# The opening of an attention and feed-forward kernel: x loaded tile by tile, normalised rows made ahead, clears and table loads moved

## The chip, the cores and the metric

The kernel runs on one core of a Trainium2 chip. The time is that of one execution on the device, in microseconds. Five engines work side by side, each with its own queue of instructions in fixed order: TensorE (PE, matmuls), VectorE (DVE), ScalarE (ACT), GpSimd (POOL) and SyncE (SP, which here issues all transfers). They wait for one another through counting semaphores.

## The reference, cut to what matters

Input x has 1024 rows of 512 floats. All arithmetic is in float32. The layer is

```
x = x + attention(layernorm(x))      # 32 heads of 128, 8 key/value heads, rotary positions, causal
x = x + ffn(layernorm(x))            # x W^T + b, and a low-rank part weighted by a router
layernorm(x) = (x - mean(x)) / sqrt(var(x) + 1e-5)
q = x w_q, k = x w_k, v = x w_v, lq = x w_lq, lk = lq w_lk, lv = x w_lv    # x here is normalised
out = softmax(mask(q k^T)) v  w_o  +  softmax(mask(q lk^T)) lv  w_lo
```

Only the first layernorm and the projections for the first head belong to the part of the program that the change touches.

## The kernel before

Every float32 operand of a matmul is split in two: a high half (a copy, made by ScalarE, written as fp32r) and a low half (the difference, made by VectorE or GpSimd). A product is three matmuls: high by low, low by high, high by high (lines 414 to 416, `mm3`). So each operand that TensorE reads has to pass ScalarE, and then VectorE or GpSimd.

The program has an opening, eight groups of four heads written out one after another, and a closing part. The order on each engine is that of the source; nothing is scheduled by a program. x lives in `acc`, 8 tiles of 128 rows (`NT` = 8, half of them is `TPC` = 4). The opening does this:

- SP issues the first half of x (`load_x(0)`, L310, 1 MB, one transfer), the identity matrix `ident`, the first weights w_q and w_k, the second half of x, then the constants cos, sin and mask (512 KB each), then w_lq, w_v, w_lk and w_lv. `load` (L321) puts weights into two slots of `stage`; from the third load on it waits until the low half made from the slot is done.
- VectorE: `statistics` (L909 to L917) of four tiles, then ScalarE's square root (`root`, L706), then `inverse_std` (L923 to L927), five tiny operations in a chain. `normalise` (L944) writes a normalised tile into `o_raw`, which has two places, and waits for the transpose that last read its place. `normalised_lo` (L950) makes the low half of the transposed tile.
- TensorE: `normalised_transpose` (L429) turns one tile into `bankT`, which has two banks, by four 128x128 transposes; from the third tile on it waits for the low half of the tile two before. ScalarE's `normalised_hi` (a copy, L701) makes the high half in `xnT`.
- Then TensorE makes eight projections of twelve matmuls each: Q, K, latent Q and V for columns 0 to 511 (n = 0), then the same for columns 512 to 1023 (n = 1). Tiles 4 and 5 are transposed after the first projection, 6 and 7 after the second. The weights' low halves come from GpSimd (`weights_low`, L1187).
- Q and K are rotated: ScalarE copies from PSUM (`rope_take`), VectorE makes two half products with sin (`rotate`, L976, L977), GpSimd a product with cos and a sum (`rope_add`, L1193, L1195), ScalarE the high half (`rope_high`), GpSimd the low one (`rope_low`, L1187). Four such rounds (p = 0 to 3) lie in the opening; the last one's low half releases the scores of the first window.
- GpSimd clears `PTD`, `OT`, `Wo` and `Wlo` (L1268) after the low halves of w_q and w_k. ScalarE's function tables are loaded where a function of another table is next in its queue: at the start, at the square root, and before the first exp (L760).

TensorE's first score tiles follow the eighth projection.

Of the kernel before, what the change touches and what calls it, by code (L numbers as in the profile page):

```python
# [10 lines left out]
ACT = mybir.ActivationFunctionType  # L11
# [89 lines left out]
def attn_ffn_kernel(nc, x_in, w_q, w_k, w_v, w_o, w_lq, w_lk, w_lv, w_out_latent, W, b, A, B, router_W, router_b,  # L101
                    cos_in, sin_in, mask_in, ident_in, pick_in,
                    averaged_in, out, inverses):
    with ExitStack() as ctx:
# [7 lines left out]
        def sem(name):  # L112
# [49 lines left out]
        x_loaded, w_loaded = [sem("x_loaded0"), sem("x_loaded1")], [sem("w_loaded0"), sem("w_loaded1")]  # L162
# [12 lines left out]
                                                  sem("cleared"))  # L175
        xn_made, xt_ready, xt_hi, xt_lo = sem("xn_made"), sem("xt_ready"), sem("xt_hi"), sem("xt_lo")
# [4 lines left out]
        f32 = lambda ap: ap.bitcast(F32)  # L181

# [124 lines left out]
        def _(sp):  # L307
            def load_x(half):
                tiles = slice(half * TPC, (half + 1) * TPC)
                sp.dma_start(acc[:, tiles, :], x_in[0, half * CH:(half + 1) * CH, :].rearrange("(i p) d -> p i d", p=P))\  # L310
                    .then_inc(x_loaded[half], 16)
# [13 lines left out]

            load_x(0)
            sp.dma_start(ident[:, :], ident_in).then_inc(ident_loaded, 16)
# [83 lines left out]
        def _(pe):  # L411
# [11 lines left out]
            def normalised_transpose(made, i):  # L423

                pe.wait_ge(xn_made, made + i + 1)
                if i >= 2:
                    pe.wait_ge(xt_lo, made + i - 1)
                for k in range(ND):
                    mm = pe.transpose(bankT[i % 2][:, k * P:(k + 1) * P],  # L429
                                      o_raw[:, i % 2, k * P:(k + 1) * P], ident[:, :])  # L430
                mm.then_inc(xt_ready, 1)
# [171 lines left out]
            for n in range(2):  # L603
                for x, weights in enumerate(places):
                    if n == 0:
                        pe.wait_ge(w_lo, x + 1)
                        pe.wait_ge(xt_lo, TPC)
                    elif x == 0:
                        pe.wait_ge(xt_lo, NT)
                    if n:  # L610

                        pe.wait_ge(*((rope_raw, x + 1) if x < 2 else (x_free, x - 1)))
                    project(weights, n, place=four[x]).then_inc(x_ready, 1)
                    if n == 0 and x < 2:
                        normalised_transpose(0, TPC + 2 * x)
                        normalised_transpose(0, TPC + 2 * x + 1)
# [81 lines left out]
        def _(act):  # L698
# [9 lines left out]
            def normalised_hi(made, tiles):  # L708
                for i in tiles:
                    act.wait_ge(xt_ready, made + i + 1)  # L710
                    copy(xnT[0][:, :, i * P:(i + 1) * P], bankT[i % 2][:, :].rearrange("p (k n) -> p k n", k=ND))\
                        .then_inc(xt_hi, 1)
# [135 lines left out]

            weights_hi(0, 0, 1, Wq)
# [4 lines left out]
            root(1, 1)  # L854

# [11 lines left out]
            normalised_hi(0, range(TPC, TPC + 2))  # L867
            weights_hi(3, 1, 2, Wv)
            first_take(0)
            normalised_hi(0, range(TPC + 2, NT))  # L870
# [33 lines left out]
        def _(dve):  # L904
            def statistics(step, half):

                tiles = range(half * TPC, (half + 1) * TPC)
                for i in tiles:
                    dve.bn_stats(stats[:, i, :], acc[:, i, :]).then_inc(dve_chain, 1)  # L909
                chain[0] += TPC  # L910
# [27 lines left out]
            def normalise(made, i):  # L938
                if i >= 2:

                    dve.wait_ge(xt_ready, made + i - 1)
                    if made:
                        dve.wait_ge(xt_used, i - 1)
                dve.tensor_scalar(o_raw[:, i % 2, :], acc[:, i, :], mv[:, i, 0:1], std[:, 2, i:i + 1],  # L944
                                  ALU.subtract, ALU.mult).then_inc(xn_made, 1)

            def normalised_lo(made, i):
                dve.wait_ge(xt_hi, made + i + 1)
                rows = slice(i * P, (i + 1) * P)
                dve.tensor_tensor(xnT[1][:, :, rows], bankT[i % 2][:, :].rearrange("p (k n) -> p k n", k=ND),  # L950
# [127 lines left out]
            dve.wait_ge(x_loaded[0], 16)  # L1078
            statistics(0, 0)
            inverse_std(0, 0)  # L1080
            normalise(0, 0)
            normalise(0, 1)
            for i in range(TPC):
                normalised_lo(0, i)
                if i < 2:
                    normalise(0, i + 2)
            dve.wait_ge(x_loaded[1], 16)
            statistics(1, 1)
            inverse_std(1, 1)
            normalise(0, 4)  # L1090
            normalise(0, 5)
# [8 lines left out]
            normalised_lo(0, 4)  # L1100
            normalised_lo(0, 5)
            rotate(0, 0, 0, 0)
            normalise(0, 6)
            normalise(0, 7)
            normalised_lo(0, 6)
            normalised_lo(0, 7)
# [78 lines left out]
        def _(pool):  # L1185
# [77 lines left out]
            weights_low(0, 0, Wq)  # L1263
            weights_low(1, 1, Wk)

            for tensor in (*PTD, *OT, *Wo, *Wlo):
                flat = tensor[tuple([ALL] * len(tensor.shape))]
                ins = pool.memset(f32(flat), 0.0)  # L1268
            ins.then_inc(cleared, 1)
            weights_low(2, 0, Wlv)  # L1270
# [55 lines left out]
```

## Time and profile before

| | us |
|---|---|
| median of 3 runs (2163.46 to 2166.22) | 2163.77 |
| the profiled execution | 2163.13 |
| its span | 2161.4 |
| TensorE busy | 2079.6 (96%) |
| VectorE busy | 1577.7 (73%) |
| ScalarE busy | 1140.6 (53%) |
| GpSimd busy | 884.0 (41%) |

The span is the time from the first to the last instruction; a busy time is the sum in which an engine had an instruction running. Of 40 equal slices of the span only the first shows TensorE at half (5 tenths), the last two at 8, all others at 9 or more.

### The profile page before, as it was taken

Reading aid. Unit: us, or ns where it says so; the run is one execution under the profiler, and the core shown is the slowest. Engines: PE = TensorE matmul, PEld = TensorE weight load, DVE = VectorE, ACT = ScalarE, POOL = GpSimd, SP = SyncE. Lnnn points to the kernel's source line nnn. Section 1 sums busy time; section 2 is a strip of 40 time slices with the busy share of each in tenths; the row PEclk is TensorE's granted clock in tenths of the full one; section 3 lists DMA queues with packets and bytes.
Section 4 is the critical chain, followed back from the end, with each engine's and each line's share of the span. In section 5 each row is a group of like instructions: output and inputs, shape, how many; then the busy total and the mean of one; then the engine's idle time right before and its main releaser. Section 6 shows DMA issues by size and latency. Waiting matters only on the chain.

```text
span 2161.4 us, 32460 instructions
## 1 busy us (share of the span) xinstructions
PE 2079.6 (96%) x11236; PEld 1757.8 (81%) x11236; DVE 1577.7 (73%) x2946; ACT 1140.6 (53%) x2502; POOL 884.0 (41%) x693
## 2 busy tenths in 40 slices
PE   5999999999999999999999999999999999999988
PEld 4888888888788888888888888888878888888877
DVE  6777777777777777777777777777777777777775
ACT  2555545555455555555455554555545555555541
POOL 4433443434533344443533344343453334444311
PEclk9999999999999999999999999999999999999999
DMA  2111111111011111111111111111211112111121
GB/s 95 36 35 37 38 30 41 41 36 45 26 41 27 40 46 30 41 32 41 36 36 35 37 38 30 41 41 37 45 26 41 27 41 46 30 41 32 41 50 39
DMA packets 101840, 83.71 MB, mean 39 GB/s; under 512 B 28200, under 2 KB 73896, under 8 KB 101680
## 3 DMA queue, kind: packets, MB, share of 16 engines
q1 hardware_dynamic: 101680, 81.65, 15.2%
q8 instruction: 91, 1.49, 0.3%
q14 instruction: 69, 0.57, 0.1%
HBM read 79.26 MB, written 2.36 MB: 38 GB/s over the span
## 4 chain that ended last, share of the span: by engine, by line
PE 76%; DVE 16%; issue 4%; ACT 3%; POOL 1%; DMA 0%; DVEq 0%; SPq 0%; ACTq 0%
PE scores L414 9%; PE scores L416 9%; PE scores L415 9%; PE bankX L414 8%; PE bankT L476 8%; PE bankX L416 8%; PE bankX L415 8%; PE bankO L414 5%; PE bankO L416 5%; PE bankO L415 5%; DVE rot_half L977 4%; DVE rot_half L976 3%; DVE probs L960 3%; DVE o_raw L1031 2%; DVE PT_lo L966 1%
## 5 line engine op out<-in xcount | busy, mean ns | idle before, releaser
L701 ACT ACTIVATE PT_hi<-bankT 128x512 fp32r<-128x512 f32 (+2 forms) x640 | 337.1, 533 | 406.4 <-PE bankO L416 341.8
L966 DVE TENSOR_TENSOR PT_lo<-bankT,PT_hi 128x512 fp32r<-128x512 f32 (+2 forms) x640 | 387.4, 609 | 197.8 <-ACT PT_hi L701 192.7
L760 ACT ACTIVATE probs<-probs,nmax 128x128 f32<-128x128 f32 (+7 forms) x512 | 394.8, 773 | 138.0 <-DVE nmax L960 137.9
L960 DVE CUSTOM_DVE_ANT_0 probs<-scores,mask 128x128 f32<-128x128 f32 (+7 forms) x512 | 381.3, 749 | 66.8 <-PE scores L416 65.6
L476 PE MATMUL bankT<-ident,probs 128*128 128x128 f32 x2304 | 379.1, 273 | 7.6 <-DVE PT_lo L966 2.0
L476 PEld LDWEIGHTS bankT<-ident,probs 128*128 128x128 f32 x2304 | 285.2, 140 | 75.6 <-DVE PT_lo L966 20.7
L1193 POOL TENSOR_TENSOR rot<-rot,cos 128x512 f32<-128x512 f32 x144 | 185.7, 1289 | 218.0 <-DVE rot_half L977 218.0
L1187 POOL TENSOR_TENSOR OT_lo<-o_raw,OT_hi 128x512 fp32r<-128x512 f32 x64 | 83.0, 1296 | 409.8 <-ACT OT_hi L701 409.8
L1195 POOL TENSOR_TENSOR rot<-rot,rot_half 128x512 f32<-128x512 f32 x144 | 207.2, 1439 | 11.3
L701 ACT ACTIVATE OT_hi<-o_raw 128x512 fp32r<-128x512 f32 x128 | 80.9, 632 | 193.7 <-DVE o_raw L1031 152.6
L976 DVE TENSOR_TENSOR rot_half<-rot,sin 64x512 f32<-64x512 f32 x144 | 108.2, 751 | 85.6 <-ACT rot L701 82.1
L977 DVE TENSOR_TENSOR rot_half<-rot,sin 64x512 f32<-64x512 f32 x144 | 159.6, 1108 | 2.0
L701 ACT ACTIVATE rot<-bankX 128x512 f32<-128x512 f32 x140 | 82.7, 591 | 120.0 <-PE bankX L416 119.1
L993 DVE TENSOR_TENSOR acc<-bankX,acc 128x512 f32<-128x512 f32 x130 | 89.9, 692 | 70.7 <-PE bankX L416 68.1
L414 PE MATMUL scores<-LKT_hi,QT_lo 128*128 128x384 f32 (+4 forms) x384 | 136.4, 355 | 5.0 <-DVE nmax L960 5.0
L414 PE MATMUL scores<-KT_hi,QT_lo 128*128 128x384 f32 (+4 forms) x384 | 134.4, 350 | 5.2 <-POOL QT_lo L1187 3.7
L414 PE MATMUL bankO<-PT_hi,LV_lo 128*128 128x512 f32 (+2 forms) x320 | 136.0, 425 | 3.4 <-DVE o_raw L1031 3.4
L414 PE MATMUL bankO<-PT_hi,V_lo 128*128 128x512 f32 (+2 forms) x320 | 135.8, 424 | 2.0
L1031 DVE TENSOR_TENSOR o_raw<-bankO,inv_b 128x512 f32<-128x512 f32 x128 | 136.5, 1066 | 0.0
L415 PE MATMUL scores<-KT_lo,QT_hi 128*128 128x384 f32 (+4 forms) x384 | 131.9, 343 | 0.0
L416 PE MATMUL scores<-LKT_hi,QT_hi 128*128 128x384 f32 (+4 forms) x384 | 131.8, 343 | 0.0
L416 PE MATMUL scores<-KT_hi,QT_hi 128*128 128x384 f32 (+4 forms) x384 | 131.6, 343 | 0.0
(241 smaller groups left out, 5197.7 us busy)
## 6 DMA issues: line engine op xcount, KB each, us to landing
inv_b<-inverses SPq DMA_DIRECT2D x128, 256.0 KB, 4.0
stage<-in_L_attn_w_q SPq DMA_DIRECT2D x32, 256.0 KB, 4.9
stage<-in_L_attn_w_lv SPq DMA_DIRECT2D x32, 256.0 KB, 2.8
stage<-in_L_attn_w_o SPq DMA_DIRECT2D x32, 256.0 KB, 5.0
stage<-in_L_attn_w_lo SPq DMA_DIRECT2D x32, 256.0 KB, 2.6
acc<-in_L_attn_hidden_states SPq DMA_DIRECT2D x2, 1024.0 KB, 6.9
stage<-in_L_attn_w_k SPq DMA_DIRECT2D x8, 256.0 KB, 5.0
stage<-in_L_attn_w_v SPq DMA_DIRECT2D x8, 256.0 KB, 5.3
```

What stands on the lines that cost most here:

```text
L414: pe.matmul(place, left[1], right[0], start=start, stop=False)
L415: pe.matmul(place, left[0], right[1], start=False, stop=False)
L416: return pe.matmul(place, left[0], right[0], start=False, stop=stop)
L476: mm = pe.transpose(bankT[j % 2][:, t * P:(t + 1) * P], probs[c][:, at:at + P], ident[:, :])
L701: return act.activation(place, src, ACT.Copy)
L760: act.activation(prob_tile(c, t), prob_tile(c, t), ACT.Exp, bias=nmax[:, c, t:t + 1], scale=-1.0, accum_out=rsum[:, c, t:t + 1]).then_inc( ...
L960: dve.tensor_tensor_reduce(place, src, tile_view(mask[:, S - width:S], c), -SCALE, -MASKED, ALU.add, ALU.min, nmax[:, c, t:t + 1]).then_in ...
L966: dve.tensor_tensor(pt_place(1, hh, w, j), bankT[j % 2][:, block_columns(c, j):CH], f32(pt_place(0, hh, w, j)), ALU.subtract).then_inc(pt_ ...
L977: dve.tensor_tensor(rot_half[HALF:HD, half, :], rot[0:HALF, slot, :], sin[0:HALF, t], ALU.mult)\
L1031: dve.tensor_tensor(o_raw[:, w % 2, :].rearrange("p (t q) -> p t q", q=P), bankO[:, :].rearrange("p (t q) -> p t q", q=P), inv_b[:, w % 2, ...
L1193: pool.tensor_tensor(rot[:, slot, :], rot[:, slot, :], cos[:, chunk(n)], ALU.mult).then_inc(rope_cos, 1)
L1195: pool.tensor_tensor(rot[:, slot, :], rot[:, slot, :], rot_half[:, half, :], ALU.add).then_inc(rope_sum, 1)
```

## The change

- SP issues the identity first, then x by tiles of 128 rows, each with a semaphore of its own: tiles 0 to 3 before w_q and w_k, tiles 4 to 7 after them.
- The eight normalised tiles of the first layernorm get eight places of their own in `probs` and four PSUM banks (`bankT` two, `bankO`, `bankX`); `normalise` waits for no transpose there, and a transpose waits for the low half four tiles before.
- VectorE takes the statistics of tiles 4 and 5 before the first `inverse_std`, of 6 and 7 after the first four normalised tiles; all of tiles 4 to 7 are normalised before the mask is copied and before the first rotation.
- TensorE transposes tiles 4 to 7 in one go after the first projection.
- GpSimd's clears come first in its queue, without `OT`, which ScalarE now clears by four copies with scale 0.
- ScalarE does a square root of one column at the start, and an exp of one column after the second root; VectorE waits for the latter before it copies the mask.

The layernorm of the closing part keeps its two places and its order.

```diff
@@ waits and places @@
+        x_banks = [bankT[0], bankT[1], bankO, bankX]
+
+        def x_normalised(made, i):
+
+            if made:
+                return o_raw[:, i % 2, :]
+            return probs[1][:, i * CH:(i + 1) * CH] if i < 6 else probs[0][:, (i - 6) * CH:(i - 5) * CH]
+
+        def x_bank(made, i):
+            return bankT[i % 2] if made else x_banks[i % TPC]
@@ SP @@
-                sp.dma_start(acc[:, tiles, :], x_in[0, half * CH:(half + 1) * CH, :].rearrange("(i p) d -> p i d", p=P))\
-                    .then_inc(x_loaded[half], 16)
+                for i in range(tiles.start, tiles.stop):
+                    sp.dma_start(acc[:, i, :], x_in[0, i * P:(i + 1) * P, :]).then_inc(x_loaded[i], 16)
...
+            sp.dma_start(ident[:, :], ident_in).then_inc(ident_loaded, 16)
             load_x(0)
-            sp.dma_start(ident[:, :], ident_in).then_inc(ident_loaded, 16)
@@ TensorE @@
-                if i >= 2:
-                    pe.wait_ge(xt_lo, made + i - 1)
+                ahead = 2 if made else TPC
+                if i >= ahead:
+                    pe.wait_ge(xt_lo, made + i - ahead + 1)
...
-                    if n == 0 and x < 2:
-                        normalised_transpose(0, TPC + 2 * x)
-                        normalised_transpose(0, TPC + 2 * x + 1)
+                    if n == 0 and x == 0:
+                        for i in range(TPC, NT):
+                            normalised_transpose(0, i)
@@ ScalarE @@
+            act.wait_ge(ident_loaded, 16)
+            act.activation(rinv[:, 0, 0:1], ident[:, 0:1], ACT.Sqrt)
+            for half in OT:
+                for kind in range(2):
+                    act.activation(half[:, kind, :], ident[:, 0:1].broadcast_to([P, S]), ACT.Copy, scale=0.0)
             weights_hi(0, 0, 1, Wq)
             weights_hi(1, 1, 1, Wk)
             root(0, 0)
             normalised_hi(0, range(TPC))
             weights_hi(2, 0, 2, Wlv)
             root(1, 1)
+            act.activation(rinv[:, 0, 1:2], ident[:, 0:1], ACT.Exp).then_inc(tables_loaded, 1)
...
-            normalised_hi(0, range(TPC, TPC + 2))
             weights_hi(3, 1, 2, Wv)
             first_take(0)
-            normalised_hi(0, range(TPC + 2, NT))
+            normalised_hi(0, range(TPC, NT))
             first_take(1)
@@ VectorE @@
-            dve.wait_ge(x_loaded[0], 16)
             statistics(0, 0)
+            tile_statistics(range(TPC, TPC + 2))
             inverse_std(0, 0)
-            normalise(0, 0)
-            normalise(0, 1)
+            for i in range(TPC):
+                normalise(0, i)
+            tile_statistics(range(TPC + 2, NT))
             for i in range(TPC):
                 normalised_lo(0, i)
-                if i < 2:
-                    normalise(0, i + 2)
-            dve.wait_ge(x_loaded[1], 16)
-            statistics(1, 1)
+            whole_statistics(1)
             inverse_std(1, 1)
-            normalise(0, 4)
-            normalise(0, 5)
+            for i in range(TPC, NT):
+                normalise(0, i)
+            dve.wait_ge(tables_loaded, 1)
             dve.wait_ge(consts_loaded, 48)
             dve.tensor_copy(mask[:, :], vT[:, :]).then_inc(mask_made, 1)
...
-            normalised_lo(0, 4)
-            normalised_lo(0, 5)
+            for i in range(TPC, NT):
+                normalised_lo(0, i)
             rotate(0, 0, 0, 0)
-            normalise(0, 6)
-            normalise(0, 7)
-            normalised_lo(0, 6)
-            normalised_lo(0, 7)
             rotate(1, 1, 0, 1)
@@ GpSimd @@
-            weights_low(0, 0, Wq)
-            weights_low(1, 1, Wk)
-
-            for tensor in (*PTD, *OT, *Wo, *Wlo):
+            for tensor in (*PTD, *Wo, *Wlo):
                 flat = tensor[tuple([ALL] * len(tensor.shape))]
                 ins = pool.memset(f32(flat), 0.0)
             ins.then_inc(cleared, 1)
+            weights_low(0, 0, Wq)
+            weights_low(1, 1, Wk)
```

## Rows read from the trace of the kernel before

**Rows 1.** Busy time by stretches: busy us (instructions) per engine, granted clock, DMA.
```profile
33.10:38.00 4.90, 1.64 (x9) 1.24 (x9) 4.63 (x5) 0.60 (x1) 2.59 (x2) 0.81 0.19 54
38.00:39.60 1.60, 1.60 (x6) 1.31 (x5) 0.67 (x2) 1.18 (x3) 0.00 (x0) 0.52 0.00 0
...
110.00:2161.00 2051.00, 1995.80 (x10823) 1688.29 (x10821) 1502.70 (x2812) 1092.10 (x2405) 839.19 (x651) 1.00 0.15 37
```
**Rows 2.** Timeline of TensorE: start us, us, then the instruction and the wait before it.
```profile
17.45 1.94 PE L429 MATMUL bankT<-ident,o_raw 128*128 128x128 f32 x8 [17.45 <-DVE o_raw L944]
...
24.07 0.76 PE L414 MATMUL scores<-xnT_hi,Wq_lo 128*128 128x512 f32 x1 [1.50 <-DVE xnT_lo L950]
...
29.32 1.04 PE L429 MATMUL bankT<-ident,o_raw 128*128 128x128 f32 x8
30.12 0.48 PE L414 MATMUL scores<-xnT_hi,Wk_lo 128*128 128x512 f32 x1
...
35.86 0.90 PE L429 MATMUL bankT<-ident,o_raw 128*128 128x128 f32 x4 [2.75 <-DVE o_raw L944]
...
44.31 0.39 PE L414 MATMUL scores<-xnT_hi,Wq_lo 128*128 128x512 f32 x1
...
54.97 0.39 PE L416 MATMUL scores<-xnT_hi,Wv_hi 128*128 128x512 f32 x1
...
61.50 0.41 PE L414 MATMUL scores<-KT_hi,QT_lo 128*128 128x320 f32 x1 [1.21 <-POOL KT_lo L1187]
```
**Rows 3.** Timeline of VectorE.
```profile
6.31 2.47 DVE L909 BATCH_NORM_STATS2 inv_b<-acc 128x6 f32<-128x512 f32 x4 [6.31 <-DMA acc<-in_L_attn_hidden_states]
...
10.46 0.18 DVE L923 RECIPROCAL inv_b<-inv_b 128x4 f32<-128x4 f32 x1 [1.03 <-ACT inv_b L706]
...
11.06 5.44 DVE L926 TENSOR_SCALAR inv_b<-inv_b 128x4 f32<-128x4 f32 x1
...
16.75 1.00 DVE L944 TENSOR_SCALAR o_raw<-acc,inv_b 128x512 f32<-128x512 f32 x2
...
30.59 1.29 DVE L950 TENSOR_TENSOR xnT_lo<-bankT,xnT_hi 128x512 fp32r<-128x512 f32 x2 [0.77 <-ACT xnT_hi L701]
...
34.22 2.99 DVE L944 TENSOR_SCALAR o_raw<-acc,inv_b 128x512 f32<-128x512 f32 x2
```
**Rows 4.** Timeline of GpSimd.
```profile
8.13 1.27 POOL L1187 TENSOR_TENSOR Wq_lo<-stage,Wq_hi 128x512 fp32r<-128x512 f32 x1 [7.69 <-ACT Wq_hi L701]
...
11.06 1.81 POOL L1268 MEMSET OT_hi<- 128x2048 f32 x1
...
15.95 0.53 POOL L1268 MEMSET Wlo_lo<- 128x512 f32 x1
...
34.26 1.26 POOL L1193 TENSOR_TENSOR rot<-rot,cos 128x512 f32<-128x512 f32 x1 [1.32 <-DVE rot_half L977]
...
55.11 1.29 POOL L1193 TENSOR_TENSOR rot<-rot,cos 128x512 f32<-128x512 f32 x1
```
**Rows 5.** The instructions on `acc` up to 60 us: the two x transfers.
```profile
L310 SPq DMA_DIRECT2D acc<-in_L_attn_hidden_states x2: 442/474/507, 0.7 to 2.8; - x2
...
DMA to landing us min/median/max: 5.5/6.9/8.2
```
**Rows 6.** DMA issues: tile, count, KB each, median us from issue to landing.
```profile
stage<-in_L_attn_w_lo SPq DMA_DIRECT2D x32, 256.0 KB, 2.6
...
stage<-in_L_attn_w_lq SPq DMA_DIRECT2D x1, 256.0 KB, 6.3
```
**Rows 7.** Timeline of ScalarE.
```profile
7.42 0.63 ACT L701 ACTIVATE Wq_hi<-stage 128x512 fp32r<-128x512 f32 x1 [5.40 <-DMA stage<-in_L_attn_w_q]
8.28 0.63 ACT L701 ACTIVATE Wk_hi<-stage 128x512 fp32r<-128x512 f32 x1 [0.23 <-DMA stage<-in_L_attn_w_k]
...
54.01 1.28 ACT L760 ACT_TABLE_LOAD   x1
```
**Rows 8.** ScalarE by line and shape over the whole span.
```profile
L760 ACT ACTIVATE probs<-probs,nmax 128x1024 f32<-128x1024 f32 x64 | 73.7, 1152 | 38.1 <-DVE nmax L960 38.1
```

More of the change, by code:

```diff
@@ L159, in attn_ffn_kernel @@
         banksX = [bankX[:, :], scores[1][:, 1, :]]
-        x_loaded, w_loaded = [sem("x_loaded0"), sem("x_loaded1")], [sem("w_loaded0"), sem("w_loaded1")]
+        x_loaded, w_loaded = [sem(f"x_loaded{i}") for i in range(NT)], [sem("w_loaded0"), sem("w_loaded1")]
         consts_loaded = sem("consts_loaded")
@@ L175, in attn_ffn_kernel @@
                                                   sem("cleared"))
+        tables_loaded = sem("tables_loaded")
         xn_made, xt_ready, xt_hi, xt_lo = sem("xn_made"), sem("xt_ready"), sem("xt_hi"), sem("xt_lo")
@@ L425, in normalised_transpose @@
                 pe.wait_ge(xn_made, made + i + 1)
-                if i >= 2:
-                    pe.wait_ge(xt_lo, made + i - 1)
+                ahead = 2 if made else TPC
+                if i >= ahead:
+                    pe.wait_ge(xt_lo, made + i - ahead + 1)
                 for k in range(ND):
-                    mm = pe.transpose(bankT[i % 2][:, k * P:(k + 1) * P],
-                                      o_raw[:, i % 2, k * P:(k + 1) * P], ident[:, :])
+                    mm = pe.transpose(x_bank(made, i)[:, k * P:(k + 1) * P],
+                                      x_normalised(made, i)[:, k * P:(k + 1) * P], ident[:, :])
                 mm.then_inc(xt_ready, 1)
@@ L710, in normalised_hi @@
                     act.wait_ge(xt_ready, made + i + 1)
-                    copy(xnT[0][:, :, i * P:(i + 1) * P], bankT[i % 2][:, :].rearrange("p (k n) -> p k n", k=ND))\
+                    copy(xnT[0][:, :, i * P:(i + 1) * P], x_bank(made, i)[:, :].rearrange("p (k n) -> p k n", k=ND))\
                         .then_inc(xt_hi, 1)
@@ L904, in _, with tile_statistics, whole_statistics @@
         def _(dve):
+            def tile_statistics(tiles):
+                for i in tiles:
+                    dve.wait_ge(x_loaded[i], 16)
+                    dve.bn_stats(stats[:, i, :], acc[:, i, :]).then_inc(dve_chain, 1)
+                chain[0] += len(tiles)
             def statistics(step, half):
+                tile_statistics(range(half * TPC, (half + 1) * TPC))
+                whole_statistics(half)
+            def whole_statistics(half):
                 tiles = range(half * TPC, (half + 1) * TPC)
-                for i in tiles:
-                    dve.bn_stats(stats[:, i, :], acc[:, i, :]).then_inc(dve_chain, 1)
-                chain[0] += TPC
                 dve.wait_ge(dve_chain, chain[0])
@@ L938, in normalise @@
             def normalise(made, i):
-                if i >= 2:
+                if i >= 2 and made:
                     dve.wait_ge(xt_ready, made + i - 1)
-                    if made:
-                        dve.wait_ge(xt_used, i - 1)
-                dve.tensor_scalar(o_raw[:, i % 2, :], acc[:, i, :], mv[:, i, 0:1], std[:, 2, i:i + 1],
+                    dve.wait_ge(xt_used, i - 1)
+                dve.tensor_scalar(x_normalised(made, i), acc[:, i, :], mv[:, i, 0:1], std[:, 2, i:i + 1],
                                   ALU.subtract, ALU.mult).then_inc(xn_made, 1)
@@ L949, in normalised_lo @@
                 rows = slice(i * P, (i + 1) * P)
-                dve.tensor_tensor(xnT[1][:, :, rows], bankT[i % 2][:, :].rearrange("p (k n) -> p k n", k=ND),
+                dve.tensor_tensor(xnT[1][:, :, rows], x_bank(made, i)[:, :].rearrange("p (k n) -> p k n", k=ND),
                                   f32(xnT[0][:, :, rows]), ALU.subtract).then_inc(xt_lo, 1)
```

## The prediction

> **What bounds the kernel now.** I read the busy table by stretches first [rows 1]. From 110 us to the end TensorE is busy 1995.8 of 2051 us: no edit of the opening can change this part, it can only begin sooner or later. So the question is how many microseconds earlier the first stretch ends. There, between 33.1 and 38.0 us, TensorE is busy 1.64 of 4.9 us. Then the timelines of single engines. TensorE [rows 2] does nothing until 17.45, starts the first projection (Q, columns 0 to 511) at 24.07, and ends the last of the eight opening projections at 54.97 + 0.23 = 55.2 (a matmul's row overlaps the next; the step is 0.23). I measure the change by what it does to this 55.2. What stands before 24.07 is VectorE's [rows 3]: statistics from 6.31, a wait of 1.03 for ScalarE's root at 10.46, and then a `tensor_scalar` on 4 columns that takes 5.44 us (11.06 to 16.50). GpSimd's timeline explains it [rows 4]: its ten operations in one unbroken run (two weight halves, eight clears) end at 15.95 + 0.53 = 16.48, and VectorE goes on at once. At 34.22 the same again: two normalisations that took 1.00 together at 16.75 take 2.99 beside GpSimd's rotary product at 34.26, and TensorE waits for them.
>
> The clock: the twelve matmuls of the first projection step by 0.4375 us ((29.32 - 24.07) / 12), later ones by 0.227 ((55.20 - 44.31) / 48) [rows 2]. The granted clock is 0.52 in 38.0 to 39.6 [rows 1], behind the gap before 35.86, and the first projection has the step that belongs to that level: so I take the two steps for the clock's two levels, 1.2 and 2.4 GHz. It rose at the end of 5.2 us of unbroken projection and fell again with the gap.
>
> **The change part by part, as a new time line.**
>
> *x in eight transfers, the identity first.* One issue costs 0.44 to 0.51 us of SP's time; the two big x transfers, issued at 0.7 and 2.8, landed 5.5 and 8.2 us later, at 6.3 and 11.0 [rows 5]. Three of the old issues become nine: six more, 2.8 us of SP's time, during which the transfers are already queued behind one another, so the bytes decide. x3 has ahead of it what the first half had, plus the identity (1/16 of it): 6.5 for 6.3. w_q and w_k keep their bytes ahead, w_k at 8.28 [rows 7]. x4 to x7 fill 8.28 to 11.0 at 0.68 each: x5 at 9.65. The three constants are issued later but have the same bytes ahead; nothing asks for them before 22 us. Bounds: a 256 KB transfer by itself lands in 2.6 us [rows 6], so 0.68 each is the lower end, and 2.6 each, one after another, the upper (rival D).
>
> *Statistics and root.* Last tile 6.5 + 0.7, aggregate and add 0.65 (8.78 to 9.43, the start of the 1.03 wait) [rows 3]: 7.85. VectorE now takes tiles 4 and 5 before it asks for the root: 9.65 + 0.7 = 10.35. ScalarE must be through by then. Its queue: root's table at the start (1.28, idle time), identity at 0.74 + 2.6 = 3.3 at the latest, a root of 0.2, then four clears of 128x1024. No such copy is in the trace; the exp of that shape takes 1.15 [rows 8], a 128x512 copy 0.63 [rows 7]; I take 1.1, so 4.4 in all, between 2.5 and 4.6. They end at 7.9 under the transfers; w_q and w_k halves end at 9.1, root at 9.3. Cover left: 1.0 us; beyond it each microsecond of clears costs one.
>
> *Inverse, without the stall.* 10.46 to 16.75 is 6.29; without the 5.44 and with 0.17 for that instruction, 1.0: 11.35. The six clears that stay on GpSimd (0.53 or less each [rows 4], 3.2 in all) now run before anything of VectorE's. The two weight halves, 8.1 to 10.6 before (1.27 each [rows 4]), shift to 8.5 to 11.0 and can still hold the short instruction for a few tenths; 0 to 0.5, I take 0.
>
> The Trainium skill (SBUF — State Buffer, "Who interferes with whom") says that whichever of a two-port VectorE operation and a GpSimd operation comes first holds the pair for one whole instruction. By that rule alone the stall would have ended with the 1.81 us clear then running, and only some 1.8 us would be there to gain; the trace shows it lasting through six clears in a row [rows 3, 4], so the row decides.
>
> *Normalise ahead.* Four at 0.5 (1.00 for two): 13.3. Statistics of tiles 6 and 7, 1.25: 14.5 (x7 is there since 11). Low halves: TensorE's transposes begin at 12.0 and take 0.24 each at the low clock (eight in 1.94 [rows 2]), so sixteen end at 15.9, and ScalarE's last high half at 16.5; VectorE's four low halves step by 0.65 (two in 1.29 [rows 3]) from 14.5: 17.1, and TensorE follows 0.15 later. The first projection begins at 17.3 instead of 24.07: 6.8 us gained. VectorE's queue sets this, not TensorE.
>
> *Second half.* Aggregate, root, inverse from 17.1: 19.2; normalise 4 to 7: 21.2. GpSimd's half of w_v (1.3, as w_q's) falls in it, since w_v's high half stands behind the exp table on ScalarE (18.2 to 20.3): up to 1.3 more, 22.5. The first projection takes 5.25 and ends at 22.55, so nothing waits, with a cover that is thin only for the first of the four. The sixteen transposes at the high clock: eight took 0.8 (29.32 to 30.12) [rows 2], so 1.6: 24.15. Then seven projections of 12 x 0.227 without a gap: 24.15 + 19.1 = 43.25. Old 55.2 less 43.25: 11.95 gained, of which 6.8 before the first projection and 5.2 in what follows it (the gap, and the clock's second fall).
>
> *Exp table early.* Its load at 54.01 [rows 7] ended at 55.29, before a score could be there (TensorE's last projection ends at 55.2): 0 gained. Early it lies on ScalarE between the second root and w_v's half, under the first projection: 0 lost. VectorE's new wait for it is passed by then; behind it stand the mask's copy and the low halves 4 to 7, due only at 32.5.
>
> *After 43.25.* GpSimd's rotary work, four rounds of 2.6 + 1.3 us with a ScalarE copy between, must keep up. Old: the fourth began at 55.11 [rows 4], 0.1 before 55.2. New: rotation 0 after the low halves, 26 to 27.5; rounds 0 and 1 end at 32.2 and 36.8; round 2 takes the second Q (35.1, copied 36.1) at 37.5 and its last part waits for the latent copy after the seventh projection (40.6), as before; round 3 begins at 43.1. The same offset, so what follows up to TensorE's wait for GpSimd at 61.50 [rows 2] moves as a block, and then the whole kernel.
>
> **Sum.** Of the profiled execution (2163.13 us; span 2161.4 and 1.7 around it): 2163.1 - 11.9 = 2151.2. The median of the runs is 0.6 above that execution; between both I say 2151.5.
>
> **Rivals.**
> A, the forecast, own range 2149.5 to 2154. Chance 0.64.
> B, the rotary rounds on GpSimd become the bound. Rotation 0 starts only 6 us earlier than before, and the rounds took 34.26 to 55.11 = 20.85 to the fourth. If collisions with VectorE (it is denser now) keep that length, the fourth begins at 27.5 + 20.85 = 48.35, 5.2 later than I say: 2156.7. Against it: most of the 20.85 was waiting. A small version is the gap in TensorE at the second transposes. 0.15.
> C, the clock rises sooner, because transposes now run unbroken into the first projection: up to 12 x 0.21 = 2.5 less, 2149.0. Against: a wait of about 1.5 us remains before 17.3. 0.08.
> D, the small transfers land one after another, 2.6 each. x5 would be the eighth after the identity: 3.3 + 7 x 2.6 = 21.5, x7 at 26.7, the three constants (twice the size) not before 36, w_lq behind them at 38.6. The second root stands behind w_lq's half on ScalarE: 39.5, normalise to 42, TensorE idle from 36 on, transposes at the low clock to 46, seven projections and their cold start to 67: 12 late, 2175. It decides from a landing distance of about 2 us. Against it: w_k landed 0.9 after w_q [rows 7], and 1 MB, four tiles' worth, behind it by 11.0. 0.03.
> E, the opening gets shorter but what stands behind it in the queues does not: w_lq lands later (6.3 from issue before [rows 6], issued when GpSimd's first half is done, about 9.8, so 16.1), and ScalarE's second root stands behind it. 1.5 us of slack, then one for one; at 9 late the gain is 3: 2160.5. 0.07.
> F, anything of the main loop that runs less well in another phase: 0.03, half of it slower.
>
> The Trainium skill (DMA: Bandwidth & Descriptors, "Measured") advises batching transfers to 1 MiB or more, giving about 2 us fixed for each. Eight loads of 256 KB go against it; read as an overlap of fixed costs it changes nothing, read as a sum it is D. The rows named under D speak for the overlap.
>
> **How the numbers follow.** Faster by over 0.2% (4.3 us, which is about what a measurement of this kernel can tell from none): A, B, C, 0.87 and a little of F: 0.88. Within 0.2%: E and a part of F, 0.08. Slower: D and the rest, 0.04. The range holds A, C and B: 2148 to 2157.5, leaving out E, D and F.
>
> **What would show it.** L926 at 0.2 instead of 5.44 us; first transposes near 12.0, first projection near 17.3, TensorE without a gap from there, the eight projections ended near 43.3; everything from the first scores on at the same distances as before. The forecast is wrong if x5 lands after 11 us, if ScalarE's clears push the root past 10.4, if the transposes of tiles 4 to 7 wait for VectorE, or if the fourth rotary round begins more than 0.3 us after the last projection.

## The result

Five runs of the changed kernel have a median of 2152.99 us (2151.65 to 2155.06), five of the kernel before, beside them, 2166.22 (2163.46 to 2167.5): a ratio of 0.994, 95% interval 0.9926 to 0.9954. The profiled execution of the changed kernel took 2152.99 us with a span of 2151.2, so 10.2 less span than the one the prediction was worked out on. That execution of before, 2163.13, lay at the low end of what later runs of it gave (2160.64 to 2168.97 in all): by medians 13.2 us are gained, by the two profiles 10.2. Part of that difference is TensorE's clock: in 46 later runs of the kernel before, those with a mean granted clock of 0.998, as in both profiles, took 2160.64 to 2164.22 us, those with 0.994 took 2167.76 to 2168.97. Among the runs at 0.998 or more the medians of the two kernels are 2163.24 (11 runs) and 2152.05 (6), 11.2 apart; whether the change makes the lower clock rarer is not shown. The forecast was 2151.5, with a range of 2148 to 2157.5.

TensorE's timeline in the changed kernel (columns as in [rows 2]; mm3 is now lines 425 to 427, the transposes L441):

```profile
12.40 1.94 PE L441 MATMUL bankT<-ident,probs 128*128 128x128 f32 x8 [12.40 <-DVE probs L967]
...
17.35 0.47 PE L425 MATMUL scores<-xnT_hi,Wq_lo 128*128 128x512 f32 x1 [1.53 <-DVE xnT_lo L973]
...
20.26 1.11 PE L441 MATMUL bankT<-ident,probs 128*128 128x128 f32 x8
...
22.58 0.66 PE L441 MATMUL bankX<-ident,probs 128*128 128x128 f32 x4 [0.76 <-DVE probs L967]
22.99 0.48 PE L425 MATMUL scores<-xnT_hi,Wk_lo 128*128 128x512 f32 x1
...
42.15 0.28 PE L425 MATMUL scores<-KT_hi,QT_lo 128*128 128x256 f32 x1
...
48.67 0.41 PE L425 MATMUL scores<-KT_hi,QT_lo 128*128 128x320 f32 x1 [1.42 <-POOL KT_lo L1205]
...
50.25 0.63 PE L426 MATMUL bankX<-lqT_lo,Wlk_hi 128*128 128x512 f32 x1
50.68 0.63 PE L427 MATMUL bankX<-lqT_hi,Wlk_hi 128*128 128x512 f32 x1
```

The first projection starts 6.7 us earlier than in [rows 2]. It takes 2.9 us (17.35 to 20.26) where it took 5.25: it already runs at the high step. TensorE waits 0.76 for the last of the second four tiles, the eight projections end at 42.15 instead of 55.2 (13.05 gained), and the wait for GpSimd's last low half ends at 48.67 instead of 61.50 (12.8). Then the two rows at 50.25 and 50.68 stand 0.43 apart: the low step is back.

VectorE's timeline shows why the first half is early and why the 0.76 is there:

```profile
9.28 1.36 DVE L925 BATCH_NORM_STATS2 inv_b<-acc 128x6 f32<-128x512 f32 x2 [0.94 <-DMA acc<-in_L_attn_hidden_states]
10.56 0.16 DVE L947 RECIPROCAL inv_b<-inv_b 128x4 f32<-128x4 f32 x1
...
11.29 0.17 DVE L950 TENSOR_SCALAR inv_b<-inv_b 128x4 f32<-128x4 f32 x1
...
11.71 1.92 DVE L967 TENSOR_SCALAR probs<-acc,inv_b 128x512 f32<-128x512 f32 x4
...
19.65 2.87 DVE L967 TENSOR_SCALAR probs<-acc,inv_b 128x512 f32<-128x512 f32 x4
```

The 5.44 us of [rows 3] are 0.17. The second four normalisations take 2.87 instead of 1.92. GpSimd's timeline shows what they met, and the end of its rotary work:

```profile
20.71 1.53 POOL L1205 TENSOR_TENSOR Wv_lo<-stage,Wv_hi 128x512 fp32r<-128x512 f32 x1 [2.38 <-ACT Wv_hi L713]
...
42.74 1.28 POOL L1205 TENSOR_TENSOR QT_lo<-rot,QT_hi 128x512 fp32r<-128x512 f32 x1 [0.74 <-ACT QT_hi L713]
43.98 1.29 POOL L1211 TENSOR_TENSOR rot<-rot,cos 128x512 f32<-128x512 f32 x1
...
47.35 1.26 POOL L1205 TENSOR_TENSOR KT_lo<-rot,KT_hi 128x512 fp32r<-128x512 f32 x1 [0.74 <-ACT KT_hi L713]
```

The last line in the kernel before:

```profile
60.17 1.27 POOL L1187 TENSOR_TENSOR KT_lo<-rot,KT_hi 128x512 fp32r<-128x512 f32 x1 [2.41 <-ACT KT_hi L701]
```

The fourth round begins at 43.98, 1.8 behind the last projection; before it was 0.1 ahead [rows 2, 4]. Before, GpSimd then waited 2.41 for ScalarE's high half; now it waits 0.74.

How far the gain reaches the end can be read at a point that each window of the main loop has: SP's store of the inverses (L340, now L351). The first two, before and after:

```profile
63.59 0.34 SPq L340 DMA_DIRECT2D inverses<-rinv  x1
...
78.28 0.33 SPq L340 DMA_DIRECT2D inverses<-rinv  x1
```
```profile
50.78 0.34 SPq L351 DMA_DIRECT2D inverses<-rinv  x1
...
67.00 0.33 SPq L351 DMA_DIRECT2D inverses<-rinv  x1
```

12.8 us are gained at the first and 11.3 at the second. What took the 1.5 is the clock, in the stretch 48.6 to 53.0 (columns as in [rows 1], granted clock third from the end):

```profile
48.60:53.00 4.40, 4.33 (x15) 3.54 (x16) 2.87 (x7) 1.63 (x4) 1.69 (x3) 0.61 0.02 0
53.00:54.50 1.50, 1.50 (x10) 1.47 (x9) 0.61 (x2) 1.19 (x3) 0.00 (x0) 1.00 0.22 51
```

After that the distance moves little: 11.2 at the 25th store, 10.7 to 11.0 from the 60th to the last (two single stores, the 48th and the 112th, stand 1.2 and 1.1 off, with no effect on their neighbours). By the output's first issue (2154.00 before, 2143.40 after) it is 10.6, and 10.2 at the end of the span. The second profile of the changed kernel (e0 below) loses as much against the same profile of before, 12.5 to 11.5; what takes this last microsecond was not looked into.

### The profile page after: what moved, and what is told of

It reads as the page before. It is cut to its first block, busy times and chain, and to the rows that moved or that the text cites. A ratio compares the mean times of both kernels' runs of the same rounds, so it can differ in the third digit from the quotient of the medians.

```text
span 2151.2 us, 32469 instructions
## 1 busy us (share of the span) xinstructions
PE 2077.0 (97%) x11236; PEld 1756.7 (82%) x11236; DVE 1572.3 (73%) x2946; ACT 1142.7 (53%) x2507; POOL 881.0 (41%) x691
## 4 chain that ended last, share of the span: by engine, by line
PE 76%; DVE 16%; issue 4%; ACT 2%; POOL 1%; DMA 0%; SPq 0%; DVEq 0%; ACTq 0%
PE bankX L425 9%; PE scores L425 9%; PE bankT L488 9%; PE scores L427 8%; PE scores L426 8%; PE bankX L427 8%; PE bankX L426 8%; PE bankO L425 5%; PE bankO L427 5%; PE bankO L426 5%; DVE rot_half L1000 4%; DVE rot_half L999 3%; DVE probs L983 3%; DVE o_raw L1054 1%; DVE PT_lo L989 1%
## 5 line engine op out<-in xcount | busy, mean ns | idle before, releaser
L1213 POOL TENSOR_TENSOR rot<-rot,rot_half 128x512 f32<-128x512 f32 x144 | 207.4, 1440 | 11.3
```

The lines of the kernel that those rows point to most:

```text
L1213: pool.tensor_tensor(rot[:, slot, :], rot[:, slot, :], rot_half[:, half, :], ALU.add).then_inc(rope_sum, 1)
```

## The experiments

Each row of the table has five to nine runs of its kernel, with the kernel before beside them on the same chip; e1, e2, e3 and e5 shared one chip, e0, e6, e7 and e8 a second, e4, e10 and e11 a third, and e12 had a fourth, so medians are compared across these groups by their ratios only. "Gain" is how much earlier than in the profile of before the first and the second store of the inverses are issued, in one profile each. "Eight end" is the start of the first score tile, which follows the eighth projection.

```
run                  first projection  eight  gain at     median   ratio (95% interval)
                     start   length    end    1st   2nd
before               24.07   5.25      55.20  -     -     -        -
after                17.35   2.91      42.15  12.8  11.3  2152.99  0.9940 (0.9926 to 0.9954)
e0_after_again       17.32   4.51      42.66  12.5  12.5  2152.36  0.9940 (0.9928 to 0.9953)
e1_clears_first      18.80   4.96      49.44   5.8   5.8  2159.08  0.9979 (0.9970 to 0.9989)
e2_clears_back       23.10   2.93      47.94   7.0   7.0  2158.58  0.9972 (0.9961 to 0.9982)
e3_x_halves          19.56   2.94      44.40  10.6  10.6  2154.55  0.9954 (0.9941 to 0.9968)
e5_two_places        20.57   4.40      48.09   7.1   5.7  2158.71  0.9973 (0.9962 to 0.9984)
e4_exp_late          17.58   4.70      43.08  12.1  12.1  2154.62  0.9948 (0.9936 to 0.9960)
e6_filler            18.09   4.33      43.24  12.0  11.8  2152.39  0.9942 (0.9930 to 0.9955)
e7_rotary_order      17.99   4.14      42.93  12.8  12.8  2151.43  0.9934 (0.9922 to 0.9947)
e8_rotary_and_wv     17.49   4.39      42.71  12.7  12.7  2151.59  0.9935 (0.9922 to 0.9949)
e10_warm             18.00   4.41      43.22  12.0  12.0  2152.36  0.9947 (0.9934 to 0.9959)
e11_warm_rotary_wv   17.64   4.21      42.86  12.6  12.6  2152.68  0.9942 (0.9930 to 0.9954)
e12_warm_kept        17.52   2.83      41.15  14.2  14.2  2150.05  0.9934 (0.9920 to 0.9947)
```

**The clears alone.** Kernel before, its eight clears ahead of GpSimd's first two weight halves:

```diff
+            (the loop of clears, PTD, OT, Wo, Wlo)
             weights_low(0, 0, Wq)
             weights_low(1, 1, Wk)
-            (the loop of clears)
```

> The kernel before with one edit: GpSimd's eight clears (OT among them) stand ahead of its first two weight halves. Theory (the 5.44 us tensor_scalar is held by the run of clears): that instruction takes 0.2 us, the first projection starts near 18.8 instead of 24.07, and everything behind it moves by the same 5.3 us: time 0.9976 of the kernel before, span near 2156. Rival (the port is a side show, the order of normalising and transposing sets the pace): under 2 us. For the clock: the transposes keep their 1 us gap in the middle; if that gap is why the first projection ran at the low clock, its step stays 0.43; if it was the position in time, it may be 0.23, and then 2.5 us more are gained.

VectorE's timeline of this run:

```profile
11.06 0.17 DVE L926 TENSOR_SCALAR inv_b<-inv_b 128x4 f32<-128x4 f32 x1
```

The instruction starts at the same 11.06 as in [rows 3] and takes 0.17. First projection 18.80, 5.3 us earlier as expected; 5.8 us gained at both stores (0.3 of it is a shorter first projection, 4.96 for 5.25). The stall is the run of clears; the rival of under 2 us is out. Here all eight clears, those of `OT` too, end on GpSimd at 6.7, before its first weight half at 8.05: that ScalarE clears `OT` in the changed kernel is not shown to be worth anything.

**The clears put back in the changed kernel** (all eight on GpSimd behind the first two weight halves, none on ScalarE).

> The changed kernel with the clears as before: all eight on GpSimd behind its first two weight halves, none on ScalarE. Theory (stall): the tensor_scalar before the reciprocal takes over 5 us again and ends near 16.5, the first projection starts near 22.5 instead of 17.35, time 5.2 us above the changed kernel. Rival (with everything normalised ahead VectorE has slack): under 2 us. For the clock: the sixteen transposes stay unbroken, so the step of the first projection is 0.23 if that is what raises the clock, and may be 0.43 if position in time does.

```profile
11.37 5.63 DVE L947 TENSOR_SCALAR inv_b<-inv_b 128x4 f32<-128x4 f32 x1
```

The stall returns at its full length, the first projection goes to 23.10 (5.75 later), and 5.8 of the changed kernel's 12.8 are lost at the first store. So this part is worth 5.3 and 5.75 at the first projection and 5.8 at the store in the two surroundings: it adds.

**x in two transfers of 1 MB, the rest of the change kept** (`load_x` as before, statistics wait for the half).

> The changed kernel with x in two transfers of 1 MB as before (identity still first). Theory (VectorE's statistics of tiles 4 and 5 stand before the first inverse and now wait for the whole second half, landed at 11.0): inverse from 12.4 instead of 10.56, first projection near 19.2 instead of 17.35, 1.8 us above the changed kernel. Rival (small transfers carry a fixed cost each, so the two large ones land sooner): the first inverse not later than 10.6 and the time equal or lower.

```profile
7.08 2.47 DVE L925 BATCH_NORM_STATS2 inv_b<-acc 128x6 f32<-128x512 f32 x4 [7.08 <-DMA acc<-in_L_attn_hidden_states]
...
11.51 1.29 DVE L925 BATCH_NORM_STATS2 inv_b<-acc 128x6 f32<-128x512 f32 x2 [0.36 <-DMA acc<-in_L_attn_hidden_states]
```

The small transfers let tiles 4 and 5 be read at 9.28 instead of 11.51. They cost nothing that shows: the first half is there at 7.08, when tile 3 of the changed kernel was there too (its statistics end at 7.7). 2.2 us gained by the tiles, as the first projection and the first store both say; 1.8 was expected.

**Two places, two banks.**

```diff
-            return probs[1][:, i * CH:(i + 1) * CH] if i < 6 else ...
+            return probs[1][:, (i % 2) * CH:(i % 2 + 1) * CH]
-            return bankT[i % 2] if made else x_banks[i % TPC]
+            return bankT[i % 2]
-                ahead = 2 if made else TPC
+                ahead = 2
```

> The changed kernel with two places and two banks for the normalised tiles, and the waits of the kernel before (order of the new kernel kept). Theory (the ring holds VectorE and TensorE in step): third tile's transpose waits for the first low half, first projection near 20.0 instead of 17.35, and a wait of about 2 us in TensorE between the first and second projection: 4.5 us above the changed kernel. Rival (VectorE's own queue of work sets the pace): under 1 us. For the clock: the transposes have a gap again; step of the first projection 0.43 if the gap matters, adding up to 2.5.

```profile
17.12 1.94 PE L441 MATMUL bankT<-ident,probs 128*128 128x128 f32 x8 [2.52 <-DVE xnT_lo L974]
20.57 0.76 PE L425 MATMUL scores<-xnT_hi,Wq_lo 128*128 128x512 f32 x1 [1.50 <-DVE xnT_lo L974]
27.96 1.22 PE L441 MATMUL bankT<-ident,probs 128*128 128x128 f32 x8 [1.95 <-DVE xnT_lo L974]
```

Both waits came where they were expected, 2.52 and 1.95 us, both for VectorE's low halves. 5.7 us lost at the first store: in the new order, in which all tiles are normalised before the first low half, the places are worth about as much as the stall. More places in the old order, or the new order by itself, were not run. The second store stands at 5.7 for 7.1 because the low step after the wait for GpSimd, seen in the changed kernel, is here too (320 columns step by 0.27 from 54.86 on, 0.15 at the high step). The three undone parts sum to 5.8 + 2.2 + 5.7 = 13.7, against 12.8 for all together; against the second profile of the changed kernel (e0, next) to 5.5 + 2.0 + 5.4 = 12.9, for 12.5.

**The changed kernel again**, as the yardstick of the next three.

> The changed kernel unaltered, as the yardstick for the runs beside it. The step to 0.43 us per matmul between 49.7 and 52.8 us (1.5 us lost) may be there or not, if it hangs on where in time the preceding wait falls; the first projection at the step of 0.23 must be there, if the unbroken transposes make it. Time 0.994 of the kernel before.

```profile
17.32 0.76 PE L425 MATMUL scores<-xnT_hi,Wq_lo 128*128 128x512 f32 x1 [1.50 <-DVE xnT_lo L973]
...
20.44 0.63 PE L426 MATMUL scores<-xnT_lo,Wq_hi 128*128 128x512 f32 x1
20.87 0.43 PE L427 MATMUL scores<-xnT_hi,Wq_hi 128*128 128x512 f32 x1
21.14 0.40 PE L425 MATMUL scores<-xnT_hi,Wq_lo 128*128 128x512 f32 x1
```

My reading of the first four runs falls here. They had shown the high step where the sixteen transposes are unbroken (changed kernel, e2, e3: 2.9 us) and the low one where they have a gap (before, e1, e5: 5.25 to 4.4). The same program now begins its first projection at the low step and changes at 20.9. Unbroken transposes alone do not decide it. But e0 ran on another chip than e1, e2, e3 and e5, and on its chip all four profiles (e0, e6, e7, e8) have the low step in the first projection: that the chip has a part in it is not excluded. The eighth projection ends 0.5 later than in the first profile, and no low step follows the wait for GpSimd: so the second store is 12.5 earlier instead of 11.3. The fourth round on GpSimd begins 0.4 behind the last projection here, not 1.8, and GpSimd's last low half waits 1.91 for ScalarE: from the first score tile to the first store it is 8.4 us, as in the kernel before (8.6 in the first profile).

**A filler in the wait for GpSimd**: sixteen more transposes of the identity, behind the first two block transposes.

> The changed kernel with sixteen additional 128x128 transposes of the identity into the unused bankO, behind the first two block transposes and ahead of the score tile that waits for GpSimd's last rotary half (46.6 to 48.67 us). They do nothing for the result. Theory (the low step at 49.7 comes from TensorE's idle stretches just before): they fill about 1.8 us of a wait that is there anyway, the low step never comes, and the time is 0 to 1.5 us below the changed kernel, according to how often that shows it. Rival (the low step is decided by something else): it stays, time equal or, where the filler ends too late, up to 0.5 us more.

No low step followed, but none did in the unaltered kernel beside it, so the run does not tell the two theories apart. The filler outlasted the wait by 0.3 (6.6 us from the first score tile to the tile behind it, for 6.3). Median as the yardstick's (2152.39 to 2152.36).

**GpSimd's order in the rotary rounds.**

```diff
             for p in range(ROPES_BEFORE):
                 rope_add(p, p % RING, p // 2, p % 2)
-                rope_low(p, ...)
+                if p < 2:
+                    low(p)
+            low(2)
+            low(3)
...
             for t in range(TPC):
+                if t == 2:
+                    first_high(3)
                 exp_tile(t, 0, t)
-            first_high(3)
```

> The changed kernel with GpSimd's product and sum of the fourth rotary round ahead of the third round's low half, and ScalarE's high half of the fourth ahead of the third exp. Theory (after the change GpSimd's rotary rounds end the opening, behind a projection phase that is over 1.9 us before the fourth round begins): the wait for the last low half ends near 47.3 instead of 48.67, 1.3 us below the changed kernel, and the low step after it may go too (1.5 more). Rival (the exp tiles and the transposes behind them set the end): 0 to 0.4 us.

TensorE's timeline of this run:

```profile
47.83 0.41 PE L425 MATMUL scores<-KT_hi,QT_lo 128*128 128x320 f32 x1
...
49.68 0.50 PE L425 MATMUL bankX<-lqT_hi,Wlk_lo 128*128 128x512 f32 x1 [0.71 <-DVE V_lo L1011]
```

The wait for GpSimd is gone: 4.9 us from the last projection to this tile instead of 6.3. But a wait of 0.71 for VectorE's low half of V takes its place, and the first store shows 12.8 for 12.5, in an opening that had begun 0.7 later (first projection 17.99 for 17.32). From the first projection to the store it is 0.9 us less than in e0, but 0.4 of it lies in a shorter first projection (4.14 for 4.51); from the first score tile to the store it is 7.9 for 8.4. Gained by the order: 0.5 us, between the theory's 1.3 and the rival's 0.4 at most. By the ratios, 0.9934 for 0.9940, it can't be told from none.

**The same, and w_v's high half behind those of tiles 4 to 7.**

> As the run with the rotary order changed, and ScalarE's high half of w_v behind the high halves of tiles 4 to 7, so that GpSimd's low half of it no longer meets VectorE's normalisations. Theory (that meeting costs 1 us on VectorE and 0.76 on TensorE): the four normalisations take 1.9 instead of 2.87 us, TensorE passes to the second projection without the wait of 0.76, the rotary rounds begin 0.9 earlier: 0.8 us below the run with the rotary order alone, 2.1 below the changed kernel. Rival (GpSimd's low half of w_v now delays the first rotary round): no gain over the rotary order alone.

No gain over the run before it (8.2 us from the first score tile to the store, for 7.9). The question was not put: with the first projection at the low step in part (4.39 us), TensorE comes to tile 7 so late that there is no wait of 0.76 to remove in either run. The last run has the case.

**The exp table where the first exp stands.**

```diff
-            act.activation(rinv[:, 0, 1:2], ident[:, 0:1], ACT.Exp).then_inc(tables_loaded, 1)
-            dve.wait_ge(tables_loaded, 1)
```

> The changed kernel without the early exp and VectorE's wait for it, so that the exp table is loaded where the first exp stands. Theory (the prediction's: the load was covered before, and its place is worth nothing): no difference within 0.5 us. Rival, from the trace of the changed kernel (the third high half of the rotary rounds now ends only at 42.7, 0.6 behind the eighth projection, and the first maximum is there at 43.3): the load runs 42.9 to 44.1, the exp tiles and the fourth round's high half behind them come up to 0.9 later, TensorE's wait for the last low half ends 0.9 later. Against that, w_v's halves move 1.5 earlier and meet other normalisations.

ScalarE's timeline:

```profile
42.46 1.28 ACT L772 ACT_TABLE_LOAD   x1
44.22 0.40 ACT L772 ACTIVATE probs<-probs,nmax 128x128 f32<-128x128 f32 x1 [0.48 <-DVE nmax L982]
```

The load ends 0.48 before the first maximum. From the first score tile to the end of the last wait it is 6.3 us with it and 6.3 in e0. So on the path the early load is worth nothing, as predicted; the rival of 0.9 is out. The ratio, 0.9948 for 0.9940, lies within the intervals; it can't show the 0.5 us that was expected as the most.

**Sixty transposes of the identity at the start**, in the wait for the first normalised tile.

> The changed kernel with sixty additional 128x128 transposes of the identity into a free bank, from the identity's landing (2.7 us) on, ahead of the first real transposes. They do nothing for the result. Theory (the clock stands at either level at 17.3 according to what TensorE did before it, and a busy TensorE from 2.7 on makes it high each time): real transposes step by 0.11, first projection by 0.227, ends near 20.1 in the profile, as in the first profile of the changed kernel and not as in the second (21.8); the first projection does not start earlier, since VectorE's low halves release it. Opening 0.3 to 1.5 us shorter than the median, spread between runs smaller. Rival (clock changes follow fixed moments, whatever is busy): the low step shows up again in the first projection.

```profile
2.64 9.33 PE L613 MATMUL scores<-ident 128*128 128x128 f32 x60 [2.64 <-DMA ident<-const_ident]
12.96 1.11 PE L441 MATMUL bankT<-ident,probs 128*128 128x128 f32 x8 [1.00 <-DVE probs L969]
...
18.00 0.62 PE L425 MATMUL scores<-xnT_hi,Wq_lo 128*128 128x512 f32 x1 [3.01 <-DVE xnT_lo L975]
```

The first half came true: eight real transposes take 1.11 instead of 1.94. The second did not: the first projection is at the low step nevertheless. VectorE releases it, so faster transposes only lengthen the wait before it, from 1.50 to 3.01; the transposes ahead of the wait are at the high step, the first matmul behind it is at the low one. Nor did the runs lie closer together (2151.61 to 2156.65).

**The same with the rotary order and the later w_v.**

> The kernel with changed rotary order and later w_v halves, and the sixty transposes of the identity at the start. Theory: with the first projection at the high step the transposes of tiles 4 to 7 follow at 20.1 without the wait of 0.76, the eighth projection ends near 41.4, the rotary rounds begin 1 us earlier than in the run without the sixty transposes: first inverses stored 13.8 us earlier than in the kernel before (12.66 without them), median near 2150.5. Rival (a wait behind takes it): as the run without them.

The same wait of 3.01; here the first projection begins high and turns low after five matmuls. No gain: the rival held.

**And with the wait filled**: 24 further transposes of the identity between the real ones and the first projection.

> As the run with sixty transposes of the identity at the start, rotary order and later w_v halves, with twenty-four more transposes of the identity between the transposes of tiles 0 to 3 and the first projection, where TensorE waits 3.0 us. Theory (the clock follows what TensorE does; the sixty alone only made the real transposes faster and the wait after them longer, 3.0 for 1.5, in which the clock fell): with the wait filled the first projection runs at the step of 0.227 throughout and ends near 20.4, the eighth near 41.5; first inverses stored 13.5 to 13.9 us earlier than in the kernel before (12.6 without), median 2150.5 to 2151.5. Rival (another chain ends the opening: normalisation on VectorE, then rotary rounds on GpSimd): eighth projection near 41.5, but the first inverses no more than 12.9 earlier and the median as before.

```profile
14.34 2.78 PE L617 MATMUL scores<-ident 128*128 128x128 f32 x24
17.52 0.47 PE L425 MATMUL scores<-xnT_hi,Wq_lo 128*128 128x512 f32 x1 [0.39 <-DVE xnT_lo L978]
```

The first projection takes 2.83 us, the eighth ends at 41.15, and the four normalisations beside it take 1.92: with w_v moved there is no wait at tile 7. Gain at the first store 14.2, at the second 14.2, more than the 13.9 I had as the upper end; the rival's 12.9 is out. Against e11, which differs by the 24 transposes alone, 1.4 us of the 1.6 gained lie in the first projection (2.83 for 4.21). That the filler made its clock high is likely and not shown: one profile on another chip than e10's and e11's, while after unfilled waits of 1.5 us the high step came three times in eleven. Its five runs lie closest together (2149.37 to 2151.06). The ratio, 0.9934, is that of e7, and its interval holds the changed kernel's 0.994, so as a whole time it is faster than before for certain, and than the changed kernel only by the traces (14.2 for 11.3 and 12.5).

## Why the prediction was right

**The stall and the first half.** Inverse at 10.56 (10.35 said), first transposes 12.40 (12.0), first projection 17.35 (17.3). The four ScalarE clears took 3.9 instead of 4.4 (they ended at 6.7) and stayed under the transfers; root ended at 9.33. That the stall ends only with the whole run of clears was read from [rows 3, 4] and is shown by e1 and e2. VectorE's queue sets the start of the first projection: e10, e11 and e12 made the transposes faster, and it came no earlier (17.5 to 18.0 for 17.3).

**The second half.** "With a cover that is thin only for the first of the four": the meeting with GpSimd's half of w_v cost 0.95 on VectorE, as allowed. It reached TensorE, 0.76 at the last tile, because the first projection ended 2.3 us earlier than said (e3, with a short one too, has the wait at 0.75; e0, with a long one, has none). This is one of the prediction's own signs of being wrong (transposes of tiles 4 to 7 that wait for VectorE); it cost the sum nothing, since the shorter projection gave more than the wait took.

**The clock.** The term was sized wrong: 5.25 for the first projection, 2.91 in the first profile. Rival C named this, with 0.08; its argument, unbroken transposes, is not enough, as e0 shows. In the eleven profiles in which the first projection follows a wait of 1.5, its length was 2.9 three times and 4.1 to 5.25 eight times; the kernel before had the longest. One program had 2.91 and 4.51, so 1.6 us of this are no property of the program; with the long one (e0) the eight projections end only 0.5 later, because the wait of 0.76 at tile 7 is gone with it. All three short ones have unbroken transposes, but so have five of the eight long ones, and those lie on other chips than e2 and e3; what decides is open. Whether 5.25 is usual for the kernel before, a single profile of it can't say (e1, with its order, had 4.96).

**After the eighth projection.** "The same offset, so what follows moves as a block" was wrong in its first part: the fourth rotary round came 1.8 behind the last projection and not 0.1 ahead. It cost 0.2 only, since before ScalarE's four exps, not GpSimd, had held the fourth high half, and that slack took the delay up. This was the second of the prediction's signs of being wrong, and in e0 it is there at 0.4 us, with nothing lost behind it. Rival B was right in a small part: GpSimd's rounds reached the end of the opening in the first profile, for 0.2 us, and another order of them and of ScalarE's exps is worth 0.5 us in e7, 0.2 to 0.3 in e8, e11 and e12, where w_v is moved too.

**The sum.** At the end of the eight projections 13.05 were gained for 11.95 said; 12.8 after the last wait; a low step of the clock took 1.5, drift in the main loop 0.5, the tail 0.6. That 10.2 comes near my 11.9 in the profiles is an error of +1.1 and one of -2.8 that I had no term for: in part luck. "What follows moves as a block, and then the whole kernel" missed by the 0.5 and the 0.6; e0, without the low step, kept 11.5 of its 12.5.

**Worth nothing:** the exp table early (e4), as said. **Not shown:** that the identity's place ahead of x, or the early table for the root, is worth anything by itself (no run changed either); that `OT` on ScalarE is (e1 speaks against it); what the new order is worth without the new places.

## What to carry to other kernels

An instruction of a few columns that takes microseconds is a wait in disguise; look at what the other engine on its port is doing from its start to its end, and move that. When an opening gets shorter, work its slowest side chain out again with the new times, since the old distances between engines were filled with slack that is now used up. Making an operation faster ahead of a wait that something else ends only lengthens the wait; on TensorE it did not keep the clock up for what followed either (4.41 and 4.21 us in e10 and e11).

## What the runs showed that was not expected

- Filled waits: with 24 transposes of the identity in the 3.0 us before the first projection it ran in 2.83 us, without them in 4.2 and 4.4, all three with the same warm start. One profile for each, the filled one on another chip.
- The step of the matmuls, not the clock column, shows the level early in a program. In the stretch 17.32 to 21.83 of e0 the column says 1.00, while two thirds of the matmuls stand 0.43 apart:

```profile
17.32:21.83 4.51, 4.51 (x12) 3.53 (x13) 4.03 (x13) 2.22 (x4) 2.13 (x2) 1.00 0.05 15
```

- Two profiles of one program differ in the opening alone by the low step in one place or another (changed kernel: 11.3 and 12.5 at the second store). A comparison of single profiles has this much play; what decides the step with equal waits ahead stays open, the chip included.
- VectorE's short `tensor_scalar` waited through six clears in a row (5.44 us before, 5.63 in e2, 0.17 in e1), each its own instruction, and never got in between; the rows of the clears overlap a little (the one at 11.06 ends at 12.87, the next starts at 12.80). The Trainium skill (SBUF — State Buffer, "Who interferes with whom") has the pair of ports held for one whole instruction; that VectorE is kept out between them too is what these runs add.
- Eight transfers of 256 KB in one queue gave nothing away against two of 1 MB. The Trainium skill (DMA: Bandwidth & Descriptors, "Measured") advises batches of 1 MiB; here, where the transfers were issued while others were still under way, e3 shows the first inverse 2.15 us behind with the large ones (12.71 for 10.56), since their reader has to wait for the whole.
